# Reordering the steps of a planned schedule: projections, hat turns, a norm chain and a table set

## The reference

```python
x = x + L0_conv(group_norm(x))      # block 0
x = x + L1_conv(group_norm(x))      # block 1
```

## Time and profile before

| | us |
| --- | --- |
| median of 3 runs | 5542.11 (5542.05 to 5542.53) |
| the profiled execution | 5550.28 |
| its span in the trace | 5548.3 |
| POOL busy in it | 4053.5 (73%) |
| DVE busy | 4494.7 (81%) |
| PE busy | 4469.9 (81%), weight loads 2004.9 (36%) |
| ACT busy | 2602.9 (47%) |

### The profile page before, as it was taken

The page is one execution under the profiler, slowest core; times in us unless marked ns, Lnnn a source line. Parts: engine busy times, 40 slices in busy tenths (PEclk is TensorE's granted clock), DMA queues, the critical chain, the costliest instruction groups (busy, mean ns, idle before and its releaser), DMA issues.

```text
span 5548.3 us, 46071 instructions
## 1 busy us (share of the span) xinstructions
PE 4469.9 (81%) x14762; PEld 2004.9 (36%) x14762; DVE 4494.7 (81%) x5306; ACT 2602.9 (47%) x3591; POOL 4053.5 (73%) x4243
## 2 busy tenths in 40 slices
PE   7587887887878888788887878788788887888874
PEld 3233333433434333343333433333343343333331
DVE  5888969789797887978889798897978879788765
ACT  4354545445445454444544454454445444445321
POOL 2677777777777777777777777777777777777776
PEclk8688878788787887878888788787878878788896
DMA  4334344353534435344353443435344353433433
GB/s 117 92 118 134 106 132 122 120 132 106 143 106 132 123 112 140 105 131 122 115 137 104 133 123 120 131 105 140 112 130 123 108 143 104 131 116 115 122 108 100
DMA packets 279695, 667.35 MB, mean 120 GB/s; under 512 B 76447, under 2 KB 116762, under 8 KB 277210
## 3 DMA queue, kind: packets, MB, share of 16 engines
q0 software_dynamic: 203328, 555.49, 33.9%
q1 hardware_dynamic: 76128, 108.93, 7.9%
HBM read 610.00 MB, written 54.12 MB: 120 GB/s over the span
## 4 chain that ended last, share of the span: by engine, by line
PE 38%; DVE 27%; POOL 18%; issue 11%; ACT 4%; DMA 2%; DVEq 0%; ACTq 0%; SPq 0%; POOLq 0%
POOL gat L507 18%; PE yo_ps L776 12%; PE tap_ps L776 7%; DVE gat L1370 6%; PE z_ps L698 6%; DVE pairs L1349 5%; DVE conv_ps L1240 5%; DVE hat_s L1397 4%; PE tap_ps L692 3%; PE conv_ps L571 2%; DMA gat<-patch_table,ixu 2%; PE conv_ps L646 2%; PE conv_ps L590 1%; DVE uc L1247 1%; PE xh_ps L758 1%
## 5 line engine op out<-in xcount | busy, mean ns | idle before, releaser
L507 POOL DMA_INDIRECT gat<-patch_table,ixu x4236 | 4045.2, 955 | 1480.6 <-issue 1264.6
L1370 DVE TENSOR_TENSOR gat<-gat,wgt_ps 128x1024 f32<-128x1024 f32 x1059 | 1283.4, 1215 | 445.1 <-DMA gat<-patch_table,ixu 438.1
L1349 DVE TENSOR_REDUCE pairs<-gat 128x256 f32<-128x1024 f32 x1024 | 1239.5, 1210 | 0.0
L776 PE MATMUL yo_ps<-hat_s,hat_image 128*128 128x512 f32 x1860 | 1009.1, 697 | 7.4 <-issue 7.4
L776 PE MATMUL tap_ps<-hat_s,hat_image 128*128 128x512 f32 x1860 | 887.2, 626 | 0.0
L692 PE MATMUL tap_ps<-ident,pairs 128*128 128x128 f32 x2048 | 393.5, 324 | 569.7 <-DVE pairs L1349 569.7
L1040 ACT ACTIVATE val<-tap_ps 128x512 f32<-128x512 f32 x512 | 303.2, 592 | 1094.8 <-PE tap_ps L692 1094.7
L776 PEld LDWEIGHTS yo_ps<-hat_s,hat_image 128*128 128x128 f32 x1860 | 418.5, 233 | 604.5 <-issue 594.5
L1240 DVE SCALAR_TENSOR_TENSOR conv_ps<-xh,kb,conv_ps 128x1024 f32<-128x1024 f32 x480 | 617.4, 1286 | 12.7
L692 PEld LDWEIGHTS tap_ps<-ident,pairs 128*128 128x128 f32 x2048 | 271.8, 163 | 884.0 <-DVE pairs L1349 709.0
L776 PEld LDWEIGHTS tap_ps<-hat_s,hat_image 128*128 128x128 f32 x1860 | 357.4, 201 | 422.2 <-issue 410.1
(11 more groups left out here) (243 smaller groups left out, 4886.5 us busy)
## 6 DMA issues: line engine op xcount, KB each, us to landing
gat<-patch_table,ixu POOLq DMA_INDIRECT x4236, 2.7
xb<-in_x SPq DMA_DIRECT2D x31, 1024.0 KB, 10.4
patch_table<-rec SPq DMA_DIRECT2D x120, 256.0 KB, 2.3
hat_image<-patch_table SPq DMA_DIRECT2D x144, 128.0 KB
out<-n_z SPq DMA_DIRECT2D x128, 128.0 KB, 2.4
patch_table<-np SPq DMA_DIRECT2D x2, 1072.5 KB
patch_table<-gat SPq DMA_DIRECT2D x8, 256.0 KB, 2.2
patch_table<-rec SPq DMA_DIRECT2D x16, 96.0 KB
```

The source lines that it names most:

```text
L507: pool.indirect_dma_start(gat[:, k, t * 2 * REC:(t + 1) * 2 * REC], None, table_rows, bass.IndirectOffsetOnAxis(ixu[:, i, k, t:t + 1], 0)) ...
L776: m = pe.matmul(hat_sums[t % 2][:, :], hat_image[:, q // NCH % 2, i, t, :], hat_s[:, i, :], start=(i == 0), stop=(i == HI - 1))
L1349: dve.tensor_reduce(total, gat[:, k, :].rearrange("p (t x c h) -> p t c x h", t=TILES, x=2, h=2), mybir.AxisListType.XY, ALU.add).then_inc ...
L1370: dve.tensor_tensor(patch, patch, wk.rearrange("p (n h) -> p n h", h=2).unsqueeze(2).to_broadcast([128, TILES * 2, C, 2]), ALU.mult).then_ ...
```

## The change

The computation is the same; only the order of steps, one PSUM bank, some waits and two table loads change.

- `project` for a pair of chunk g's rows runs at the end of chunk g (at 9 taps, ahead of `hat_post 3`, since the chunk's own plan is merged first) instead of one tap into chunk g+1. `residual` moves from 3 taps to 2.
- The hat's turns `hat_up` 0 to 3 go from 1, 3, 5, 7 taps to 1, 2, 4, 6, `hat_post` 0 to 2 from 4, 6, 8 to 3, 5, 7; `hat_post 3` stays at 9. `hat_y` goes from 1 tap to 0.
- The norm chain moves from chunk 7 into chunk 6, `hidden 0` and `hidden 1` to the end of chunk 6, `hidden 2` and `hidden 3` to 2 and 4 taps of chunk 7; before they stood at 6, 7, 8 and 9 taps of chunk 7. `x_stats` moves ahead into chunk 5. In chunk 6 `to_table 7`, `offsets 3` and most `points` come one or two taps later. The small products take the bank `tap_ps[1]`, with waits to match.
- In the start of the program, chunk 1 of image 0 gets its offsets, pixels and points ahead of image 1's `hidden`, and DVE makes the points ahead of the kernels. The plans of image 0's first chunks are now the general ones with image 0's own steps merged in.

```diff
-PLAN_FIRST = ((2, "convolve 0"), (3, "convolve 1"), (5, "convolve 2"), (6, "exp"), (7, "ln"), (8, "tanh"))
-PLAN_BLOCK0 = ((1, "project"), (3, "residual"), (3, "convolve 0"), (4, "convolve 1"), (5, "convolve 2"), (6, "exp"),
-               (7, "ln"), (8, "tanh"), (8, "finish"))
+PLAN_FIRST = ((2, "convolve 0"), (3, "convolve 1"), (5, "convolve 2"), (6, "exp"), (7, "ln"), (8, "tanh"), (KK, "project"))
+PLAN_BLOCK0 = ((2, "residual"), (3, "convolve 0"), (4, "convolve 1"), (5, "convolve 2"), (6, "exp"), (7, "ln"), (8, "tanh"), (8, "finish"), (KK, "project"))
...
-PLAN_NORM = ((1, "project"), (3, "residual"), (4, "group_mean"), (5, "group_var"), (6, "normalise"), (8, "finish"))
+PLAN_NORM = ((2, "residual"), (4, "group_mean"), (5, "group_var"), (6, "normalise"), (8, "finish"))
 PLAN_PREPARE = (
-    ((1, "last_row"), (1, "offsets 0"), (2, "to_table 0"), (2, "x_stats 0"), (3, "to_table 1"), (4, "offsets 1"), (4, "to_pixels 0"),
-     (5, "to_table 2"), (5, "x_stats 1"), (6, "to_table 3"), (7, "to_pixels 1"), (8, "to_table 4"), (8, "finish")),
-    ((1, "offsets 2"), (2, "to_table 5"), (2, "points 0"), (3, "offsets 3"), (3, "to_pixels 2"), (4, "points 1"), (4, "to_table 6"),
-     (5, "x_stats 2"), (5, "to_table 7"), (6, "points 2"), (6, "to_pixels 3"), (7, "x_stats 3"), (8, "finish")),
-    ((1, "x_mean"), (1, "points 3"), (2, "x_var"), (2, "points 4"), (2, "next_indices"), (3, "x_norm"), (3, "points 5"),
-     (4, "hidden_units"), (5, "kernel_taps"), (6, "kernels"), (6, "hidden 0"), (7, "hidden 1"), (8, "hidden 2"), (8, "finish"), (KK, "hidden 3")),
+    ((1, "last_row"), (1, "offsets 0"), (2, "to_table 0"), (2, "x_stats 0"), (3, "to_table 1"), (4, "offsets 1"), (4, "to_pixels 0"), (4, "x_stats 1"),
+     (5, "to_table 2"), (6, "x_stats 2"), (6, "to_table 3"), (7, "to_pixels 1"), (8, "to_table 4"), (8, "finish"), (KK, "x_stats 3")),
+    ((1, "x_mean"), (1, "offsets 2"), (2, "x_var"), (2, "to_table 5"), (3, "x_norm"), (3, "points 0"), (4, "hidden_units"), (4, "offsets 3"),
+     (4, "to_pixels 2"), (5, "points 1"), (5, "kernel_taps"), (5, "to_table 6"), (6, "kernels"), (6, "to_table 7"), (7, "points 2"), (7, "to_pixels 3"),
+     (8, "hidden 0"), (8, "finish"), (KK, "hidden 1")),
+    ((1, "points 3"), (2, "next_indices"), (2, "hidden 2"), (3, "points 4"), (4, "hidden 3"), (5, "points 5"), (8, "finish")),
 )
-PLAN_HAT = ((1, "hat_rows"), (1, "hat_up 0"), (3, "hat_up 1"), (4, "hat_post 0"), (5, "hat_out 0"), (5, "hat_up 2"), (6, "hat_post 1"),
-            (7, "hat_out 1"), (7, "hat_up 3"), (8, "hat_post 2"), (KK, "hat_post 3"))
-PLAN_NEXT_HAT = ((1, "hat_y"), (3, "hat_part"), (4, "hat_x"), (6, "hat_mask"), (8, "hat_weigh"), (KK, "hat_select"))
+PLAN_HAT = ((1, "hat_rows"), (1, "hat_up 0"), (2, "hat_up 1"), (3, "hat_post 0"), (4, "hat_up 2"), (5, "hat_out 0"), (5, "hat_post 1"),
+            (6, "hat_out 1"), (6, "hat_up 3"), (7, "hat_post 2"), (KK, "hat_post 3"))
+PLAN_NEXT_HAT = ((0, "hat_y"), (3, "hat_part"), (4, "hat_x"), (6, "hat_mask"), (8, "hat_weigh"), (KK, "hat_select"))
...
-            return (tap_ps[0], tap_ps[1])[n] if isinstance(n, int) and n < 2 else tr_ps
+            return tap_ps[0] if is_first(n) else tap_ps[1]
...
-                    pe.wait_ge(rec_done, n * NCH + 1)
+                    pe.wait_ge(hat_scaled, HT * hats_before((n - 1) * NCH - 2))
...
+                if t == 1 and q % NCH == NCH - 1 and q // NCH + 2 < B:
+                    pe.wait_ge(kernel_dve, (q // NCH + 2) * KERNEL_STEPS + 8)
...
+            offsets(0, 1, 1)
             x_mean(1)
             x_var(1)
+            first_pixels(0, 1)
             x_norm(1)
             hidden_units(1)
             kernels(1)
...
             for s in range(NCH // 2):
                 hidden(1, s)
-            offsets(0, 1, 1)
-            first_pixels(0, 1)
...
-                steps = {"project": lambda b, g, i: project(b + 1, g - 1),
+                steps = {"project": lambda b, g, i: project(b + 1, g),
...
                 if n > 0:
+                    act.preload_act_table_set("silu_and_others")
                     act.wait_ge(ln_done, n * NCH + s * 2 + 2)
...
+                if s == 0:
+                    act.preload_act_table_set("silu_and_others")
```

More of the change, by code:

```diff
@@ L58 @@
 PLAN_START = (
[L59 to L62, removed]
@@ L63 @@
-    ((1, "project"), (3, "residual"), (3, "convolve 0"), (4, "convolve 1"), (5, "convolve 2"), (6, "exp"), (6, "first_points 4"),
-     (7, "ln"), (8, "tanh"), (8, "finish")),
+    ((2, "first_offsets 2"), (4, "first_offsets 3"), (5, "first_pixels 1"), (6, "first_offsets 4"), (6, "first_points 2"), (8, "first_offsets 5"),
+     (KK, "first_pixels 2")),
+    ((3, "first_offsets 6"), (4, "first_offsets 7"), (5, "first_pixels 3"), (6, "first_points 3")),
+    ((6, "first_points 4"),),
 )
-PLAN_NORM = ((1, "project"), (3, "residual"), (4, "group_mean"), (5, "group_var"), (6, "normalise"), (8, "finish"))
+PLAN_NORM = ((2, "residual"), (4, "group_mean"), (5, "group_var"), (6, "normalise"), (8, "finish"))
@@ L115, in plan_of @@
 def plan_of(b, g):
[L117 to L120, removed]
+    if g < 4:
+        plan = PLAN_BLOCK0 if g > 0 else PLAN_FIRST
+        if b == 0 and g < len(PLAN_START):
+            plan = by_unit(plan, PLAN_START[g])
     else:
@@ L822, in _ @@
             first_table(7)
+            pe.wait_ge(rec_done, ACT_COPIES[NCH - 1] + REC0)
+            pe.wait_ge(rec_dve, len(BY_DVE))
+            offsets(0, 1, 1)
             x_mean(1)
             x_var(1)
+            first_pixels(0, 1)
             x_norm(1)
@@ L827, in _ @@
             kernels(1)
-            pe.wait_ge(rec_done, ACT_COPIES[NCH - 1] + REC0)
-            pe.wait_ge(rec_dve, len(BY_DVE))
             for s in range(NCH // 2):
                 hidden(1, s)
-            offsets(0, 1, 1)
-            first_pixels(0, 1)
             def image(b, more, further):
-                steps = {"project": lambda b, g, i: project(b + 1, g - 1),
+                steps = {"project": lambda b, g, i: project(b + 1, g),
                          "group_mean": lambda b, g, i: group_mean(b + 1), "group_var": lambda b, g, i: group_var(b + 1),
@@ L894, in hidden @@
                         act.wait_ge(conv_sum, (n - 1) * CONV_SUMS)
-                if n > 1:
+                if n > 0:
                     if s == 0:
@@ L1110, in _ @@
             first_index(0)
+            offsets(0, 1, 1)
             x_var(1)
+            first_pixels(0, 1)
             x_norm(1)
             hidden_units(1)
+            first_index(1)
             for s in range(NCH // 2):
                 hidden(1, s)
-            offsets(0, 1, 1)
-            first_pixels(0, 1)
-            first_index(1)
             def image(b, more, further):
@@ L1473, in _ @@
             x_norm(1)
+            first_points(1)
             kernels(1)
-            for s in range(NCH // 2):
-                hidden(1, s)
-            first_points(1)
             dve.sem_inc(math, 2 * MATH_STEPS)
@@ L1482, in image @@
                 steps = {"convolve": lambda b, g, i: convolve(b + 1, g, i),
-                         "project": lambda b, g, i: project(b + 1, g - 1),
+                         "project": lambda b, g, i: project(b + 1, g),
                          "residual": lambda b, g, i: residual(b + 1, g - 1), "group_mean": lambda b, g, i: group_mean(b + 1),
```

## The result

The changed kernel is **slower**: 5724.62 us (5721.82 to 5726.68), against 5542.32 us for the kernel before on the same chip, a ratio of 1.0328 with a 95% interval of 1.0315 to 1.0340. The forecast was 5584 with a range up to 5690: the sign was right, the size was four times too small, and the time lies above the range. The nearest of the written cases is the far end of rival A2, 5720.

What follows compares the result with a forecast made beforehand. POOL's 4236 gathers, a chain of 5310 us, bound the kernel, with at most 95 us of waits to win. Waits of 9.1 instead of 5.5 us an image, times 14, less 8, gave +42: 5584 us, range 5458 to 5690.

Steps and rivals of the forecast that it cites:

- rival A2: Half of chunk 6's idle filled, finish's wait kept, slow clock at chunk ends: 5681, far end 5720; chance 0.17.
- The balance: Per image, DVE's lag at chunk 0 plus growth in chunks 0 to 3, less 29.0 us, is POOL's wait.
- Part 1: Project at its own chunk's end, turns earlier: chunks 0 to 3 grow 2.3 us per image, ends -2.3 and +6.9.
- I take 5.1 us for hat_up 3: PE's hat_up 3 at a chunk's end, between 4.56 (clock 1.00) and 6.29 (clock 0.50): transposes 0.3 us later.
- Rival D: Lag at chunk 0 as forecast, but the fast clock at each chunk's end: 5520; chance 0.13.
- Part 2: Norm chain and two hidden steps into chunk 6: its last product 5.6 us late, DVE's lag at chunk 0 21.9.
- filling is partial: PE's idles in chunk 6 absorb part of the added 9.9 us, so its last product is 5.6 us late.
- Rival B: Chunk 6 absorbs the chain, PE having more room than busy time shows: 5502, or 5460; chance 0.25.
- The tolerance: The lag of DVE behind the gathers that POOL bears before it waits for transposes: 29.0 us, from image 7.
- Part 3: Image 0: chunk 1's offsets go ahead of hidden, 14 us earlier; -8 us in all, between -14 and 0.
- At nothing: Table loads, hat_y at 0, x_stats in chunk 5, bank change, added waits and later to_table: counted as 0 us.
- rival F: Table loads, 89 of 1.28 us, were on the path at chunk ends, so POOL's waits go: 5460; chance 0.05.

Runs made afterwards that it cites:

- the best version: The kernel before with the new hat_up and hat_post taps and the new order of the program's start: 5462.0 us, ratio 0.9860.
- b_turns: The kernel before with the new taps of hat_up and hat_post alone: 5481.8 us, ratio 0.9893.
- b_chain: The kernel before with only the norm chain, two hidden steps and x_stats moved ahead, bank and waits with them: 5594.1 us, ratio 1.0087.
- e_up3_late: The changed kernel with hat_up 3 at 7 taps instead of 6, behind pair 2's transposes on PE: 5602.2 us, ratio 1.0123.
- b_start: The kernel before with the new order of the program's start alone: 5520.0 us, ratio 0.9960.
- both pairs: Hand-placed table loads out of or in the changed kernel, 5721.1 and 5724.6 us; the kernel before with new turns and start, 5462.0 and 5464.9.

## Why the prediction was wrong, step by step

**The balance held in image 7.** What bounds the kernel, the bound on the gain (95 us; the best version got 80) and the sum per image were right: lag plus growth less the old tolerance gives 18.3 where 20.3 were measured, and 14 images of the difference give the time.

**Part 1, the growth in chunks 0 to 3: right mechanism, mis-sized.** Forecast +2.3, measured +6.9 (181.4 against 174.4). DVE waits for Tanh at project, as forecast. The step that failed is "I take 5.1 us for hat_up 3". In the four chunks of image 7 it took 4.56, 6.89, 5.64 and 6.71, in the mean 5.95; by the prediction's own sum this is 3.4 of the missing 4.6, and the other 1.2 I can't name. That the slow end was met to the tenth is luck, since it put hat_up 3 at 6.29 in all four.

Below stand PE's idle time ahead of pair 1 in chunk 1 of the kernel before; then, of the changed kernel, the same place, hat_up 3 in chunks 0, 2 and 3, and two stretches of chunk 1 (PE, weight loads, DVE, ACT, POOL busy, then the clock), ahead of hat_up 3 and through it.

```profile
2584.54 1.11 PE L692 MATMUL tap_ps<-ident,pairs 128*128 128x128 f32 x4 [5.70 <-DVE pairs L1349]
```

```profile
2656.16 1.12 PE L689 MATMUL tap_ps<-ident,pairs 128*128 128x128 f32 x4 [3.35 <-DVE pairs L1351]
...
2617.08 4.56 PE L775 MATMUL tap_ps<-hat_s,hat_image 128*128 128x512 f32 x10
...
2708.54 5.64 PE L775 MATMUL tap_ps<-hat_s,hat_image 128*128 128x512 f32 x10
...
2754.18 6.71 PE L775 MATMUL tap_ps<-hat_s,hat_image 128*128 128x512 f32 x10
...
2659.80:2661.60 1.80, 1.43 (x7) 0.29 (x4) 1.80 (x4) 1.48 (x2) 1.50 (x2) 0.50 0.41 121
2661.60:2668.50 6.90, 6.90 (x13) 2.80 (x11) 6.90 (x8) 2.06 (x2) 5.00 (x6) 0.65 0.34 104
```

In chunk 1 the granted clock was 0.50, the lower of its two levels, ahead of hat_up 3 and 0.65 through it, after PE had idled for 3.35 us ahead of pair 1's transposes. I had argued that hat_up 2 would fill that idle; it filled part, and 3.35 of 5.70 us were left. Rival D, which bet on the full clock, came true in chunk 0 alone (4.56). And the prediction missed a version inside its own argument: with project left where it was, the same late Tanh would have been free, and the turns alone worth 61 us (b_turns). It had priced two moves as one.

**Part 2, the lag at chunk 0: mis-sized, by its lateness in chunk 6, and with the wrong limit.** The last product of chunk 6 came 18.3 us behind the first gather of chunk 7 (2542.39 against 2524.10), where it had come 8.4 (2468.33 against 2459.92): +9.9, where I had taken 5.6. These 4.3 us are nearly all of the 4.5 by which the lag was wrong. The step that failed is "filling is partial", the reckoning of idle time against work as though PE's queue were the only limit. Before and then after: chunk 7's first gather, chunk 6's last product, and PE's stretch from the end of chunk 5's last product to the end of chunk 6's.

```profile
2459.92 0.95 POOL L507 DMA_INDIRECT gat<-patch_table,ixu  x1 [0.30 <-issue]
2468.33 1.12 PE L698 MATMUL z_ps<-val,w_in 64*64 64x256 f32 x4 [0.87 <-ACT val L1044]
...
2426.09:2469.45 43.36, 36.80 (x140) 15.92 (x140) 33.88 (x48) 17.78 (x30) 33.00 (x35) 0.66 0.54 142
```

```profile
2524.10 1.09 POOL L504 DMA_INDIRECT gat<-patch_table,ixu  x1 [0.30 <-issue]
2542.39 1.12 PE L695 MATMUL z_ps<-val,w_in 64*64 64x256 f32 x4 [0.87 <-ACT val L1046]
...
2490.28:2543.51 53.23, 43.79 (x171) 20.98 (x170) 38.41 (x60) 25.03 (x40) 40.43 (x43) 0.66 0.54 143
```

PE worked 7.0 us more there (43.79 against 36.80) and stood idle for 2.9 us more (9.44 against 6.56). So none of the idle was filled; it grew. That the sum is 9.9, the end called "none filled", is luck: that end had the work at 9.9, with both hidden steps ahead of the last product, where only hidden 0 came, and no new idle. The reading of the earlier trace rows misled, too. Its stretch follows POOL's gathers of chunk 6; it begins while PE still works on chunk 5 and ends before the idle of 3.47, so PE was less full in its chunk 6 than 42.72 of 45.80.

The idle grew because the chain went round three engines (timeline of the changed kernel):

```profile
2492.43 6.96 PE L643 MATMUL conv_ps<-np,w_om 128*41 128x512 f32 x24
2499.32 0.38 PE L533 MATMUL tap_ps<-sq,pair 64*128 64x1 f32 x2
...
2505.03 0.26 ACT L877 ACTIVATE std<-tap_ps,eps_c 128x1 f32<-128x1 f32 x1
2505.32 0.16 DVE L1192 RECIPROCAL mr<-std 64x1 f32<-64x1 f32 x1 [8.03 <-ACT std L877]
2505.73 0.58 PE L538 MATMUL tap_ps<-dev,w_in 64*128 64x1 f32 x2 [4.91 <-DVE dev L1194]
```

PE makes the square root's input behind the matmuls of offsets 2, and ScalarE does the square root behind the whole evacuation of offsets 2 and a table load. Meanwhile DVE waits 8.03 us, with its multiplies queued behind, and PE 4.91 in turn. The prediction had named ScalarE in half a sentence ("the chain's steps alternate") and priced none of it. Rival B fell: PE had the room that it bet on, and the chunk did not absorb the chain, which costs 51 us by itself (b_chain). The Trainium skill, "Trainium Kernel Development and Optimization", section Performance Expectations, calls the weight loads' busy share a good measure of how close a kernel is to roofline, and matmul busy time a bad one. By that, their 20.98 of 53.23 us tell that PE had room; the trace agrees, with 9.44 us of idle, and the chain was late all the same.

In chunk 7, what was shed came back in part as new idles: hidden 1, 2 and 3 waited 2.16, 1.89 and 1.52 us for ScalarE's normalised input, hidden 2's behind hat_rows. hat_up 3 ended 18.7 us behind chunk 0's first gather instead of 14.0, +4.7 where I had -0.7. The step from there to the first multiply, forecast +2.0, was +1.2.

**The tolerance** was 27 and not 29 us: POOL now waited in chunk 0 as well (3.7 us in image 7, by its gaps), for transposes of chunk 7, which the balance leaves out. In other kernels with such waits it is lower still: in the mean of images 1 to 13 of e_up3_late, 24.4 + 170.4 - 160.5 - 10.3 = 24.0.

**Part 3, image 0**: forecast -8, ends -14 and 0; its waits fell by 16, and b_start measured 23 us, both beyond the end of -14. The convolution did wait for hidden, 14.9 us once, but not long enough to matter to POOL.

**At nothing**: right for the tables; rival F is refuted by both pairs. The Trainium skill, "ScalarE: Activation LUTs", section What ACT_TABLE_LOAD costs, adds a drain of some 1.38 us to each load's 1.28; no such drain shows in the rows of a chunk's end above, where Ln starts 0.01 us behind its load's end and Tanh likewise.

**The range** failed because growth and lag both came out near their slow ends, and the prediction, which had written 5720 for that case, left it outside. That the time came within 5 us of it is luck in part, as both sizes were met by other sums than those written down. Whether the two terms share a cause no run shows.
